# One product of layer 1 as a pair of row tiles in the middle of the layer: a layer norm, edge sum and MLP kernel on one Trainium2 core

## The chip, the cores and the metric

The kernel runs on one core of one Trainium2 chip, and the metric is the device time in microseconds of one execution. The engines are TensorE (PE in the profile, PEld its weight loads), VectorE (DVE), ScalarE (ACT), GpSimd (POOL) and SyncE (SP), which issues the DMAs. Each has its own stream of instructions; they meet at semaphores.

## The reference

12,500 nodes have 128 features each, and 200,000 edges, sorted by their destination, have 48. All is float32.

```
h    = relu(layernorm(x))
agg  = segment_sum(edge_attr, dst, 12500)          # 48 per node
c    = concat([h, agg], axis=1)                    # 176 per node
c    = silu(c @ W1 + b1)                           # W1: 176 x 256
c    = silu(c @ W2 + b2)                           # W2: 256 x 256
out  = x + h + c @ W3 + b3                         # W3: 256 x 128
```

## The kernel before

The nodes are worked on in NT = 28 tiles of 448 nodes (TILE); the last has 404. The MLP is computed with the features on the partitions and the nodes as columns, so a matmul of layers 1 and 2 has 448 columns. Layer 1 and 2 have 256 outputs, which are M = 2 blocks of 128, each in a PSUM bank of its own (`z[:, 0]` and `z[:, 1]`); both layers use the same two banks.

Layers 1 and 2 are computed in fp32r, a shorter form of float32. Each operand is therefore split in a high part, rounded to fp32r, and the rest, its low part, and three products are summed: high by high, low by high, high by low. For the node features that is L1054 to L1056. The edge sums have 48 rows only. Their high part lies in rows 0 to 47 of `agg_hilo` and their low part in rows 64 to 111 (ROW2 = 64), so one matmul of 112 rows with `w1e_hi`, which stands in both places, does two of the three products (L1059). The third one, W1's low part by the high part of the sums, is L1060: it takes the same 112 rows of `agg_hilo`, and `w1e_lo` is zero in all rows but 0 to 47. Layer 1 of a tile is thus five matmuls for each bank, ten in all.

The edges are summed per node by matmuls with a one-hot tile (`sum_tile`): each has 128 edges on the rows, 48 columns of weights (the edge features) and 42 columns of output. They come in pairs in different column tiles of the array: L1024 writes partitions 0 to 47 of `agg_ps`, L1027 partitions 64 to 111 of `stage`. A tile of nodes has 28 such pairs for each half of its groups, 56 in all.

The order on each engine is written out by hand. In step i TensorE does, one behind the other:

- layer 2 of tile i-2 (L1074 to L1078), which waits for h1_hi and h1_lo of that tile,
- layer 1 of tile i-1 (L1054 to L1060); the first matmul of each bank waits until ScalarE has read layer 2's sums out of it (semaphore `s_h2`), and L1059 of the first bank for the low part of the edge sums (`s_agg_lo`),
- the edge sums of tile i+1 (L1024, L1027),
- layer 3 of tile i-2 (L1092), then the transposes of tile i's normalized features (L1038).

ScalarE does in step i: `split_agg(i-1)` (L534, the high part of the sums), `stage_sums(i)` (L489), `relu(i-1)` (L528), `activate2(i-2, 0)` (L552, the Silu of layer 2's first bank), the clearing of a bank (L466), `activate2(i-2, 1)`, `activate1(i-1)` (L560 and L564, twice), the seeding of z3 with b3 (L541) and `normalize(i)` (L520, four pieces). VectorE does the sum of the agg parts (L849), the low parts (L859, L866, L873), the one-hot tiles (L705), the statistics and the output. GpSimd adds the staged sums (L443) and computes rstd.

Before the loop VectorE makes the low parts of the weights (`weights_lo`, L723), three subtractions; layer 1 of tile 0 waits for them (`s_w_lo`).

Of the kernel before, what the change touches and what calls it, by code (L numbers as in the profile page):

```python
# [26 lines left out]
ACT = mybir.ActivationFunctionType  # L27
AX = mybir.AxisListType
F32 = mybir.dt.float32
F32R = mybir.dt.float32r  # L30
# [3 lines left out]
def gnn_kernel(nc, x, dst, edge_attr, W1, b1, W2, b2, W3, b3, out):  # L34
    N, D = x.shape
    E, ED = edge_attr.shape
    HID = W1.shape[1]
    P = 128
    M = HID // P
    EPS = 1e-5  # L40

    PER = 4
# [6 lines left out]
    TILE = NPG * GPT  # L49
    TP = TILE // PER  # L50
    NT = -(-N // TILE)
# [11 lines left out]
    ROW2 = 64  # L63
# [23 lines left out]
    def nodes_p(t):  # L87
        return LAST_P if isinstance(t, int) and t == NT - 1 else TP

    with ExitStack() as ctx:  # L90
        def sb(name, shape, dt=F32):
            return ctx.enter_context(nc.sbuf_tensor(name, shape, dt))

        def ps(name, shape, dt=F32):
            return ctx.enter_context(nc.psum_tensor(name, shape, dt))

        def sem(name):
            return ctx.enter_context(nc.semaphore(name))


        w1x_hi = sb("w1x_hi", [D, HID], F32R)
        w1x_lo = sb("w1x_lo", [D, HID], F32R)
        w1e_hi = sb("w1e_hi", [ROW2 + ED, HID], F32R)
        w1e_lo = sb("w1e_lo", [ROW2 + ED, HID], F32R)
# [52 lines left out]
        hT_hi = sb("hT_hi", [D, TILE], F32R)  # L157
        hT_lo = sb("hT_lo", [D, TILE], F32R)
        agg = sb("agg", [ED, TILE])
        agg_hilo = sb("agg_hilo", [ROW2 + ED, TILE], F32R)  # L160
        h = sb("h", [P, 2 * M, TILE])
        h1, h2 = h[:, 0:M], h[:, M:2 * M]
        h1_hi = sb("h1_hi", [P, M, TILE], F32R)
# [8 lines left out]
        w1e_in = load_w[0:ROW2 + ED, (M + 1) * HID:(M + 2) * HID]  # L172
# [13 lines left out]
        z = ps("z", [P, M, BANK])  # L186
# [44 lines left out]
        s_agg = sem("agg_ready")  # L231
        s_agg_hi = sem("agg_hi_ready")
        s_agg_lo = sem("agg_lo_ready")
        s_w_hi = sem("weights_hi_ready")
        s_w_lo = sem("weights_lo_ready")
        s_carried = sem("overhang_carried")
# [7 lines left out]
        s_xn = sem("xn_ready")  # L244
# [5 lines left out]
        s_z1 = sem("z1_ready")  # L250
# [4 lines left out]
        s_h2 = sem("h2_ready")  # L255
# [6 lines left out]
        def wait(eng, s, count):  # L262

            if isinstance(count, int) and count <= 0:
                return
            eng.wait_ge(s, count)
# [21 lines left out]
        def has(i, lag, count):  # L288

            return not isinstance(i, int) or 0 <= i - lag < count  # L290

        def slot_turn(i, slot, slots=2):

            return (i - slot) // slots + 1
# [169 lines left out]
        def _(act):  # L464
            def clear_bank(k):
                act.activation(agg_ps[0:ED, k, :], zeros[0:ED, :].broadcast_to([ED, BANK]),  # L466
                               ACT.Copy).then_inc(s_clear, 1)
# [16 lines left out]
            def stage_sums(t, parity):  # L484

                act.wait_ge(s_summed, t + 1)
                if not isinstance(t, int) or t > 1:
                    act.wait_ge(s_added, added(t - 1))
                act.activation(staged[:, parity].rearrange("d k w -> d (k w)"),  # L489
                               stage[ROW2:ROW2 + ED, 0:STAGED],  # L490
                               ACT.Copy).then_inc(s_staged, 1)
# [16 lines left out]
            for a in (0, ROW2):  # L508
                act.activation(w1e_hi[a:a + ED, :], w1e_in[a:a + ED, :], ACT.Copy).then_inc(s_w_hi, 1)

            def normalize(i, turn):

                np_ = nodes_p(i)
                parity = turn % 2
                act.wait_ge(s_x[turn], 16 * slot_turn(i, turn, XSLOTS) + (16 if np_ != TP else 0))
                act.wait_ge(s_nmr, i + 1)
                wait(act, s_tp, i - 1)
                wait(act, s_plain, i - 1)
                for q in range(PER):
                    ln = act.activation(xn[0:np_, parity, q, :], x_t[0:np_, turn, q, :], ACT.Identity,  # L520
                                        bias=nmr[0:np_, parity, q:q + 1], scale=rstd[0:np_, parity, q:q + 1])
                ln.then_inc(s_xn, 1)

            def relu(t):
                n = PER * nodes_p(t)
                act.wait_ge(s_tp, t + 1)
                wait(act, s_z1, M * t)
                act.activation(hT_hi[:, 0:n], tp[:, 0:n], ACT.Relu).then_inc(s_hT, 1)  # L528

            def split_agg(t):  # L530
                n = PER * nodes_p(t)
                act.wait_ge(s_agg, t + 1)
                wait(act, s_z1, M * t)
                act.activation(agg_hilo[0:ED, 0:n], agg[:, 0:n], ACT.Copy).then_inc(s_agg_hi, 1)  # L534

            def seed_b3(t):

                np_ = nodes_p(t)
                act.wait_ge(s_begun, 1)
                wait(act, s_out, t)  # L540
                act.activation(z3[0:np_, :, :], b3r[0:np_, :].unsqueeze(1).broadcast_to([np_, PER, D]),  # L541
                               ACT.Copy).then_inc(s_seeded, 1)
# [23 lines left out]
            def step(i, turn):  # L566
                parity = turn % 2
                if has(i, 1, NT):
                    split_agg(i - 1)
                if has(i, 0, NT) and not (isinstance(i, int) and i == 1):  # L570
                    stage_sums(i, parity)
                if has(i, 1, NT):
                    relu(i - 1)
                last = isinstance(i, int) and i >= NT - 1
                if last and i == NT + 1:
                    seed_b3(i - 2)
                if has(i, 2, NT):
                    activate2(i - 2, 0)
                if last and i <= NT:
                    seed_b3(i - 2)  # L580
                if has(i, 1, NT - 2):
                    act.wait_ge(s_carried, i)
                    clear_bank(1 - parity)
                if has(i, 2, NT):
                    activate2(i - 2, 1)
                if has(i, 1, NT):
                    activate1(i - 1)
                if has(i, 2, NT) and not last:
                    seed_b3(i - 2)
                if has(i, 0, NT) and not (isinstance(i, int) and i == NT - 1):  # L590
                    normalize(i, turn)
                if isinstance(i, int) and i == NT - 2:
                    normalize(i + 1, (turn + 1) % XSLOTS)

            clear_carry(2)
            normalize(0, 0)
            stage_sums(1, 1)
            pipeline(act, step)

        @block.vector  # L600
        def _(dve):
# [113 lines left out]
            def weights_lo():  # L715
                dve.wait_ge(s_w_hi, 4)
                dve.wait_ge(s_pool_zero, 4)
                for lo, whole, hi in (
                        (w2_lo[:, :, :].rearrange("p m n -> p (m n)"), w2_in.rearrange("p m n -> p (m n)"),
                         w2_hi[:, :, :].rearrange("p m n -> p (m n)")),  # L720
                        (w1x_lo[:, :], w1x_in, w1x_hi[:, :]),
                        (w1e_lo[0:ED, :], w1e_in[0:ED, :], w1e_hi[0:ED, :])):
                    dve.tensor_tensor(lo, whole, hi.bitcast(F32), ALU.subtract).then_inc(s_w_lo, 1)  # L723

            dve.wait_ge(s_small0T, 1)
# [213 lines left out]
        def _(pe):  # L939
# [102 lines left out]
            def layer1(t):  # L1042

                n = PER * nodes_p(t)
                pe.wait_ge(s_hT_lo, t + 1)
                if isinstance(t, int) and t == 0:
                    pe.wait_ge(s_w_lo, 3)
                    pe.wait_ge(s_w_hi, 4)
                    pe.wait_ge(s_weights, WEIGHTS)
                    pe.wait_ge(s_const, CONSTS)  # L1050
                for m in range(M):
                    cols = slice(m * P, (m + 1) * P)
                    wait(pe, s_h2, M * (t - 1) + m + 1)
                    pe.matmul(z[:, m, 0:n], w1x_hi[:, cols], hT_hi[:, 0:n], start=True, stop=False)  # L1054
                    pe.matmul(z[:, m, 0:n], w1x_lo[:, cols], hT_hi[:, 0:n], start=False, stop=False)  # L1055
                    pe.matmul(z[:, m, 0:n], w1x_hi[:, cols], hT_lo[:, 0:n], start=False, stop=False)  # L1056
                    if m == 0:
                        pe.wait_ge(s_agg_lo, t + 1)
                    pe.matmul(z[:, m, 0:n], w1e_hi[:, cols], agg_hilo[:, 0:n], start=False, stop=False)  # L1059
                    pe.matmul(z[:, m, 0:n], w1e_lo[:, cols], agg_hilo[:, 0:n],  # L1060
                              start=False, stop=True).then_inc(s_z1, 1)

            def layer2(t, b):

# [64 lines left out]
            for c in range(FULL_ROWS):  # L1129
                pe.matmul(invalid_sum[:, 0:1], g["invalid"][:, c:c + 1], one[:, :],  # L1130
                          start=(c == 0), stop=(c == FULL_ROWS - 1))
            pe.matmul(invalid_sum[:, 1:2], g["invalid"][0:LAST_G, FULL_ROWS:ROWS], one[0:LAST_G, :],
                      start=True, stop=True, skip_group_check=True).then_inc(s_smallT, 1)
# [26 lines left out]
```

## Time and profile before

| | |
|---|---|
| median of 3 runs | 301.86 us (301.55 to 302.54) |
| the profiled execution's own time | 301.52 us |
| its span, first to last instruction | 299.8 us |
| busy share of the span: PE, PEld, DVE, ACT, POOL | 94%, 86%, 83%, 76%, 38% |
| mean granted TensorE clock | 0.983 |

All durations of the trace are from that one execution. Matmuls are pipelined: the record of one overlaps that of the next, and their ends are modelled, so the distance of the starts tells what one costs. The idle time of an engine that isn't the bound costs nothing.

### The profile page before, as it was taken

The page shows a single profiled execution, that of the slowest core. Times are in us where ns is not written, and L with a number is a line of the kernel's source. Part 1 is how long each engine was busy: PE and PEld are TensorE (multiplying, and loading weights), DVE is VectorE, ACT ScalarE, POOL GpSimd, SP SyncE. Part 2 cuts the span into 40 slices and gives each one's busy share as a digit, 9 for nine tenths or more (in the row PEclk, how much of TensorE's full clock was granted, in tenths as well). Part 3 has the DMA queues.
Part 4 walks back from the last instruction along what each step waited for, and adds up shares of the span by engine and source line. Part 5 has one row for each costly group of instructions (what it writes and reads, how often), then busy time and mean ns, then how long its engine had stood idle before and what let it go on. Part 6 is the DMA issues. An engine that isn't in the chain of part 4 may idle for free.

```text
span 299.8 us, 12214 instructions
## 1 busy us (share of the span) xinstructions
PE 282.7 (94%) x4378; PEld 258.8 (86%) x4379; DVE 249.6 (83%) x617; ACT 229.3 (76%) x435; POOL 113.8 (38%) x241
## 2 busy tenths in 40 slices
PE   6791998999999999999999999999999999999995
PEld 5681888899999999999999999999999999999794
DVE  7878897799888998889988898889988889875551
ACT  8773586787788877888778887888777887789662
POOL 3053554243433435334353334434444343532200
PEclk9888799999999999999999999999999999999999
DMA  6999076368655686557855678556875568731112
GB/s 164 303 286 254 4 218 181 94 191 245 209 155 159 215 245 191 157 151 235 245 170 150 178 237 237 158 156 184 244 230 159 147 200 245 205 104 33 33 32 58
DMA packets 79226, 52.94 MB, mean 177 GB/s; under 512 B 2949, under 2 KB 78815, under 8 KB 79205
## 3 DMA queue, kind: packets, MB, share of 16 engines
q1 hardware_dynamic: 79205, 52.70, 61.0%
q8 instruction: 8, 0.13, 0.2%
q14 instruction: 13, 0.11, 0.1%
HBM read 46.29 MB, written 6.40 MB: 176 GB/s over the span
## 4 chain that ended last, share of the span: by engine, by line
PE 81%; issue 5%; ACT 3%; DVE 3%; DMA 2%; POOL 2%; SPq 1%; POOLq 0%; ACTq 0%; DVEq 0%
PE agg_ps L1024 19%; PE z L1092 17%; PE z L1074 7%; PE z L1078 7%; PE z L1075 7%; PE z L1054 4%; PE stage L1027 4%; PE z L1056 4%; PE z L1059 4%; PE z L1060 4%; PE z L1055 4%; PE tp L1038 3%; DMA raw<-in_edge_attr_dram 2%; POOL agg_carry L443 2%; ACT xn L520 1%
## 5 line engine op out<-in xcount | busy, mean ns | idle before, releaser
L443 POOL TENSOR_TENSOR agg_carry<-staged,agg_carry 48x42 f32 x196 | 71.8, 366 | 90.8 <-ACT staged L489 61.2
L1024 PEld LDWEIGHTS agg_ps<-onehot,raw 128*48 128x48 f32 x1560 | 73.2, 126 | 9.4 <-issue 9.4
L1027 PE MATMUL stage<-onehot,raw 128*48 128x42 f32 x1568 | 77.2, 215 | 3.2 <-DMA raw<-in_edge_attr_dram 1.9
L705 DVE TENSOR_TENSOR onehot<-window,rel 128x1176 f32<-128x1176 f32 (+1 forms) x57 | 76.9, 1351 | 3.9 <-DVE stats L680 2.7
L1024 PE MATMUL agg_ps<-onehot,raw 128*48 128x42 f32 x1560 | 77.0, 215 | 0.0
L1027 PEld LDWEIGHTS stage<-onehot,raw 128*48 128x48 f32 x1568 | 73.6, 126 | 3.0 <-issue 3.0
L426 POOL TENSOR_TENSOR rstd<-vareps,minus_half 112x4 f32<-112x4 f32 (+1 forms) x28 | 38.8, 1384 | 75.9 <-DVE vareps L690 75.9
L1092 PE MATMUL z<-w,h 128*112 128x128 f32 (+1 forms) x448 | 55.9, 278 | 0.8 <-ACT h L552 0.8
L1092 PEld LDWEIGHTS z<-w,h 128*112 128x112 f32 (+1 forms) x448 | 50.4, 176 | 2.4 <-ACT z L548 1.1
L552 ACT ACTIVATE h<-z,b2c 128x448 f32<-128x448 f32 (+1 forms) x56 | 35.5, 634 | 20.0 <-PE z L1078 17.2
L520 ACT ACTIVATE xn<-x_t,nmr,rstd 112x128 f32<-112x128 f32 (+1 forms) x112 | 45.6, 478 | 0.5 <-DVE nmr L698 0.5
L560 ACT ACTIVATE h<-z,b1c 128x448 f32<-128x448 f32 (+1 forms) x56 | 35.0, 626 | 14.0 <-PE z L1060 14.0
L1074 PE MATMUL z<-h_hi,w_hi 128*128 128x448 f32 (+1 forms) x112 | 43.2, 386 | 0.0
L1075 PE MATMUL z<-h_hi,w_lo 128*128 128x448 f32 (+1 forms) x112 | 40.9, 365 | 0.0
L873 DVE TENSOR_TENSOR h_lo<-h,h_hi 128x448 fp32r<-128x448 f32 (+1 forms) x56 | 34.9, 623 | 6.5 <-ACT h_hi L564 4.9
L849 DVE TENSOR_TENSOR agg<-agg_ps,agg_carry 48x448 f32<-48x448 f32 (+1 forms) x28 | 17.2, 615 | 19.8 <-PE stage L1027 18.9
L564 ACT ACTIVATE h_hi<-h 128x448 fp32r<-128x448 f32 (+1 forms) x56 | 32.3, 576 | 1.8
L1078 PE MATMUL z<-h_lo,w_hi 128*128 128x448 f32 (+1 forms) x112 | 31.8, 365 | 0.0
L1054 PE MATMUL z<-hT_hi,w1x_hi 128*128 128x448 f32 (+1 forms) x56 | 21.3, 381 | 6.6 <-DVE hT_lo L866 6.0
L534 ACT ACTIVATE agg_hilo<-agg 48x448 fp32r<-48x448 f32 (+1 forms) x28 | 16.0, 573 | 13.4 <-DVE agg L849 13.4
L680 DVE BATCH_NORM_STATS2 stats<-x_t 112x6 f32<-112x128 f32 (+1 forms) x112 | 24.2, 278 | 0.0
L1078 PEld LDWEIGHTS z<-h_lo,w_hi 128*128 128x128 f32 x112 | 21.1, 188 | 1.8
(122 smaller groups left out, 427.5 us busy)
## 6 DMA issues: line engine op xcount, KB each, us to landing
raw<-in_edge_attr_dram SPq DMA_DIRECT2D x55, 672.0 KB, 6.0
x_t<-in_x_dram SPq DMA_DIRECT2D x27, 224.0 KB, 6.1
out_dram<-out_t SPq DMA_DIRECT2D x27, 224.0 KB, 6.0
dst_rows<-in_dst_dram SPq DMA_DIRECT2D x1, 512.0 KB
raw<-in_edge_attr_dram SPq DMA_DIRECT2D x1, 288.0 KB, 3.5
dst_rows<-in_dst_dram SPq DMA_DIRECT2D x1, 256.0 KB, 2.7
out_t<-in_L_gnn_W_dram SPq DMA_DIRECT2D x1, 256.0 KB, 7.3
x_t<-in_x_dram SPq DMA_DIRECT2D x1, 192.0 KB
```

What stands on the lines that cost most here:

```text
L426: pool.tensor_tensor(rstd[0:np_, parity], vareps[0:np_, :], minus_half[0:np_, :], ALU.pow).then_inc(s_rstd, 1)
L443: pool.tensor_tensor(into, staged[:, parity, n, :], into, ALU.add).then_inc(s_added, 1)
L520: ln = act.activation(xn[0:np_, parity, q, :], x_t[0:np_, turn, q, :], ACT.Identity, bias=nmr[0:np_, parity, q:q + 1], scale=rstd[0:np_, p ...
L552: act.activation(h2[:, m, 0:n], z[:, m, 0:n], ACT.Silu, bias=b2c[:, m:m + 1]).then_inc(s_h2, 1)
L560: act.activation(h1[:, m, 0:n], z[:, m, 0:n], ACT.Silu, bias=b1c[:, m:m + 1]).then_inc(s_h1, 1)
L705: return dve.tensor_tensor(onehot[:, slot, at * PER:n * PER, :], window[:, :].unsqueeze(1).broadcast_to([P, cols_n, WINDOW]), cols.unsquee ...
L1024: mm = pe.matmul(banks[0:ED, bass.ds(offsets[at - first], WINDOW)], edges, into, start=False, stop=True, skip_group_check=True, tile_posit ...
L1027: mm = pe.matmul(stage[ROW2:ROW2 + ED, at * WINDOW:(at + 1) * WINDOW], edges, into, start=(at == 0 and j == 0), stop=True, skip_group_chec ...
L1074: pe.matmul(z[:, m, 0:n], w2_hi[:, k, cols], h1_hi[:, k, 0:n], start=(k == 0), stop=False)
L1075: pe.matmul(z[:, m, 0:n], w2_lo[:, k, cols], h1_hi[:, k, 0:n], start=False, stop=False)
L1078: mm = pe.matmul(z[:, m, 0:n], w2_hi[:, k, cols], h1_lo[:, k, 0:n], start=False, stop=(k == M - 1))
L1092: mm = pe.matmul(into[0:np_], h2[:, k, q * np_:(q + 1) * np_], w3[:, k, :], start=False, stop=(k == M - 1), skip_group_check=True)
```

## The change

For all tiles but the last, the two L1060 matmuls (one for each bank) are replaced by two matmuls of 48 rows each, which are placed one behind the other in the middle of the layer. The first, at rows 0 to 47 (tile position (0, 0)), closes the first bank's sum. The second, at rows 64 to 111 (tile position (64, 0)), opens the second bank's, so that its L1054 no longer has `start=True`, and L1059 closes that bank. The second needs the sums' high part in rows 64 to 111, so ScalarE writes another copy of it (`agg_hi_again`, tile `agg_hi_below`), behind relu, and VectorE writes `w1e_lo` there too. TensorE waits for that copy, and for both banks, ahead of the pair. The parameter `quarters` of `normalize` and the variable `first` change nothing in what is issued. The last tile keeps its two full matmuls; rows 64 to 111 of its `w1e_lo` are no longer zero, so that it adds the product of the two low parts as well.

```diff
@@ weights_lo @@
-                        (w1e_lo[0:ED, :], w1e_in[0:ED, :], w1e_hi[0:ED, :])):
+                        (w1e_lo[0:ED, :], w1e_in[0:ED, :], w1e_hi[0:ED, :]),
+                        (w1e_lo[ROW2:ROW2 + ED, :], w1e_in[ROW2:ROW2 + ED, :], w1e_hi[ROW2:ROW2 + ED, :])):
@@ ScalarE @@
+            def agg_hi_again(t):
+                n = PER * nodes_p(t)
+                act.wait_ge(s_agg, t + 1)
+                wait(act, s_z1, M * t)
+                act.activation(agg_hi_below[ROW2:ROW2 + ED, 0:n], agg[:, 0:n], ACT.Copy).then_inc(s_agg_below, 1)
...
                 if has(i, 1, NT):
                     relu(i - 1)
...
+                if has(i, 1, NT - 1):
+                    agg_hi_again(i - 1)
@@ layer1 @@
+                last = isinstance(t, int) and t == NT - 1
                 pe.wait_ge(s_hT_lo, t + 1)
                 if isinstance(t, int) and t == 0:
-                    pe.wait_ge(s_w_lo, 3)
+                    pe.wait_ge(s_w_lo, 4)
...
                 for m in range(M):
                     cols = slice(m * P, (m + 1) * P)
                     wait(pe, s_h2, M * (t - 1) + m + 1)
-                    pe.matmul(z[:, m, 0:n], w1x_hi[:, cols], hT_hi[:, 0:n], start=True, stop=False)
+                    pe.matmul(z[:, m, 0:n], w1x_hi[:, cols], hT_hi[:, 0:n], start=(m == 0 or last), stop=False)
...
-                    pe.matmul(z[:, m, 0:n], w1e_hi[:, cols], agg_hilo[:, 0:n], start=False, stop=False)
-                    pe.matmul(z[:, m, 0:n], w1e_lo[:, cols], agg_hilo[:, 0:n],
-                              start=False, stop=True).then_inc(s_z1, 1)
+                    mm = pe.matmul(z[:, m, 0:n], w1e_hi[:, cols], agg_hilo[:, 0:n],
+                                   start=False, stop=(m == 1 and not last))
+                    if m == 1 and not last:
+                        mm.then_inc(s_z1, 1)
+                    if last:
+                        pe.matmul(z[:, m, 0:n], w1e_lo[:, cols], agg_hilo[:, 0:n],
+                                  start=False, stop=True).then_inc(s_z1, 1)
+                    elif m == 0:
+                        pe.wait_ge(s_agg_below, t + 1)
+                        wait(pe, s_h2, M * (t - 1) + 2)
+                        pe.matmul(z[:, 0, 0:n], w1e_lo[0:ED, 0:P], agg_hilo[0:ED, 0:n],
+                                  start=False, stop=True, tile_position=(0, 0)).then_inc(s_z1, 1)
+                        pe.matmul(z[:, 1, 0:n], w1e_lo[ROW2:ROW2 + ED, P:2 * P], agg_hi_below[ROW2:ROW2 + ED, 0:n],
+                                  start=True, stop=False, tile_position=(ROW2, 0))
```

## Rows read from the trace of the kernel before

**Rows 1.** The page: granted TensorE clock in 40 slices; ScalarE's copy L534 (busy, mean ns).

```profile
PEclk9888799999999999999999999999999999999999
...
L534 ACT ACTIVATE agg_hilo<-agg 48x448 fp32r<-48x448 f32 (+1 forms) x28 | 16.0, 573 | 13.4 <-DVE agg L849 13.4
```

**Rows 2.** The page: the chain that ended last, by engine.

```profile
PE 81%; issue 5%; ACT 3%; DVE 3%; DMA 2%; POOL 2%; SPq 1%; POOLq 0%; ACTq 0%; DVEq 0%
```

**Rows 3.** That chain in time order, 140 to 175 us: start, us, what.

```profile
146.93 0.20 PE z L1054
...
156.41 0.20 PE z L1054
...
158.86 0.04 PE agg_ps L1024
```

**Rows 4.** Waits of TensorE: us in total, times, longest.

```profile
PE z L1054 <- DVE hT_lo L866: 6.0, 2, 5.6
...
PE z L1054 <- ACT h L552: 0.6, 1, 0.6
```

**Rows 5.** Timeline of TensorE's matmuls, layer 1 into the edge sums: start, us.

```profile
156.86 0.36 PE L1059 MATMUL z<-agg_hilo,w1e_hi 112*128 112x448 f32 x1
...
157.28 0.37 PE L1054 MATMUL z<-hT_hi,w1x_hi 128*128 128x448 f32 x1
...
157.90 0.37 PE L1059 MATMUL z<-agg_hilo,w1e_hi 112*128 112x448 f32 x1
158.10 0.36 PE L1060 MATMUL z<-agg_hilo,w1e_lo 112*128 112x448 f32 x1
158.39 0.24 PE L1024 MATMUL agg_ps<-onehot,raw 128*48 128x42 f32 x1
158.40 0.24 PE L1027 MATMUL stage<-onehot,raw 128*48 128x42 f32 x1
```

**Rows 6.** Timeline of the weight loads in the same stretch.

```profile
157.14 0.19 PEld L1054 LDWEIGHTS z<-hT_hi,w1x_hi 128*128 128x128 f32 x1
...
157.90 0.19 PEld L1060 LDWEIGHTS z<-agg_hilo,w1e_lo 112*128 112x128 f32 x1
158.39 0.12 PEld L1024 LDWEIGHTS agg_ps<-onehot,raw 128*48 128x48 f32 x1 [0.30 <-issue]
```

**Rows 7.** Timeline, the edge sums into layer 3.

```profile
151.42 0.21 PE L1027 MATMUL stage<-onehot,raw 128*48 128x42 f32 x1
151.56 0.17 PEld L1092 LDWEIGHTS z<-w,h 128*112 128x112 f32 x1
```

**Rows 8.** Timeline, the first matmuls of layer 2.

```profile
153.69 0.19 PEld L1074 LDWEIGHTS z<-h_hi,w_hi 128*128 128x128 f32 x1
153.80 0.19 PEld L1075 LDWEIGHTS z<-h_hi,w_lo 128*128 128x128 f32 x1
154.00 0.37 PE L1075 MATMUL z<-h_hi,w_lo 128*128 128x448 f32 x1
```

**Rows 9.** Timeline near the start: transposes of 128 rows, then of 7.

```profile
16.80 0.39 PE L947 MATMUL z<-ident,rel_rows 128*128 128x128 f32 x2
...
16.91 0.28 PE L947 MATMUL z<-ident,rel_rows 128*128 128x128 f32 x1
17.11 0.19 PEld L947 LDWEIGHTS tp<-ident,rel_rows 7*128 7x128 f32 x1
```

**Rows 10.** The chain in time order, 21 to 34 us.

```profile
22.92 0.34 DVE w1e_lo L723
...
31.22 0.37 PE z L1060
```

**Rows 11.** Layer 1 of tile 0 as a window: us, engines busy (x), granted clock, DMA.

```profile
29.40:34.50 5.10, 5.10 (x12) 3.76 (x12) 5.07 (x9) 2.18 (x4) 3.74 (x4) 0.56 0.03 8
```

**Rows 12.** Timeline of ScalarE, layer 2's second Silu.

```profile
156.45 0.64 ACT L552 ACTIVATE h<-z,b2c 128x448 f32<-128x448 f32 x1
```

**Rows 13.** Waits of ScalarE: us in total, times, longest.

```profile
ACT h L552 <- PE z L1078: 17.2, 25, 0.7
```

More of the change, by code:

```diff
@@ L160, in gnn_kernel @@
         agg_hilo = sb("agg_hilo", [ROW2 + ED, TILE], F32R)
+        agg_hi_below = sb("agg_hi_below", [ROW2 + ED, TILE], F32R)
         h = sb("h", [P, 2 * M, TILE])
@@ L233, in gnn_kernel @@
         s_agg_lo = sem("agg_lo_ready")
+        s_agg_below = sem("agg_hi_below_ready")
         s_w_hi = sem("weights_hi_ready")
@@ L509, in _, with normalize @@
                 act.activation(w1e_hi[a:a + ED, :], w1e_in[a:a + ED, :], ACT.Copy).then_inc(s_w_hi, 1)
-            def normalize(i, turn):
+            def normalize(i, turn, quarters=range(PER)):
                 np_ = nodes_p(i)
@@ L518, in normalize @@
                 wait(act, s_plain, i - 1)
-                for q in range(PER):
+                for q in quarters:
                     ln = act.activation(xn[0:np_, parity, q, :], x_t[0:np_, turn, q, :], ACT.Identity,
                                         bias=nmr[0:np_, parity, q:q + 1], scale=rstd[0:np_, parity, q:q + 1])
-                ln.then_inc(s_xn, 1)
+                if quarters[-1] == PER - 1:
+                    ln.then_inc(s_xn, 1)
             def relu(t):
@@ L573, in step @@
                     relu(i - 1)
+                first = isinstance(i, int) and i == 1
                 last = isinstance(i, int) and i >= NT - 1
+                if has(i, 1, NT - 1):
+                    agg_hi_again(i - 1)
                 if last and i == NT + 1:
```

## The prediction

> **What bounds the kernel now.** I read the page first: TensorE's granted clock is full in all slices but the first few [rows 1]. A high busy share alone wouldn't make it the bound, so the chain that ended last came next: 81% of it is TensorE [rows 2]. In time order, in the middle of the run [rows 3], it is nothing but matmuls. One tile takes 9.48 us there (L1054 at 146.93 and at 156.41). The waits of TensorE say the same from the other side: for h it waits once, 0.6 us, and the large wait, 5.6 us for hT_lo, is at the start [rows 4]. So whatever the stream of TensorE gains or loses in layer 1 arrives in the end in full, 27 times (28 tiles, the last keeps its old form). ScalarE and VectorE matter only where they would come late for TensorE.
>
> The records of matmuls are 0.36 us long and overlap; what a matmul costs is the distance of starts, 0.20 us for 448 columns, with its weight load beside the matmul ahead of it [rows 5, 6]: the load for L1060 starts at 157.90, with L1059's matmul.
>
> **The change part by part.** Removed: in each of 27 tiles the two full L1060 matmuls. Added: one pair of 48-row tiles, at rows 0 and 64, in different banks. If the pair runs as one matmul, and nothing else changes, a tile saves one step of 0.20 us.
>
> But the pair stands between full matmuls, and the trace shows what happens where the shape in use changes. From L1060 (full) to L1024 (tiles of 48 columns): the weights aren't loaded beside the last full matmul; the load starts at 158.39, 0.29 behind that matmul's start at 158.10, where 0.20 would be the end of its columns [rows 5, 6]. The other way, L1027 to L1092: load at 151.56, 0.14 behind a start whose own columns take some 0.04 [rows 3, 7]. So either way costs 0.09 to 0.10 us of nothing, and then the weight load lies bare. Its price: at 153.69 and 153.80 two loads of 128 columns follow one another at 0.11, and the second matmul then starts at 154.00, 0.20 behind the second load [rows 8]; a bare load costs 0.11. Are tiles of rows like that too? The nearest row is the transposes of 7 rows near the start: the last one with 128 rows starts at 16.91, the load for the first with 7 rows at 17.11, 0.20 later, although the 128-row ones stand 0.11 apart, 16.80 to 16.91 [rows 9]. That is the same gap of 0.09. I take that a pair of 64-row tiles pays it on entry and on exit. The Trainium skill (TensorEngine Tiling (Array Packing), Key Properties) says that a change of tiling mode, unlike a change of tile, drains TensorE; by that rule the gap is paid twice here, as in my sum. By the speedup of up to 2x that the same page gives for a contraction of 64 or less (Theoretical Speedup) alone, a tile would save its 0.20 us, 5.3 us in 26 tiles. The trace agrees with the drain for tiles of columns (0.09) and shows no 64-row tile.
>
> The sum for a tile at full clock, from L1059's start (m = 0) to the start proper of L1054 (m = 1): 0.29 to the pair's weight load; 0.11 for the load; 0.01 by which the second tile stands behind the first (L1024 and L1027 start 0.01 apart [rows 5]; at most 0.11, if the two loads go one after the other); 0.29 from the pair's start to the next full weight load, as at L1060; 0.11 for that load. Together 0.81. Before it is 0.42 (156.86 to 157.28). That is 0.39 more, and L1060 of m = 1 is gone, 0.21 less: **+0.18 us a tile**, with the serial loads +0.28, and 0.31 if the dispatch behind a semaphore adds the 0.03 by which L1054's load stands further ahead of its matmul after a wait (157.14 to 157.28 [rows 5, 6]). 26 tiles give 4.7 us (to 8.1).
>
> The 27th is tile 0. Its matmuls run at a granted clock of 0.56, that is mostly at the lower of the two levels, 1.2 GHz, behind a wait of 5.6 us, and stand 0.37 apart [rows 4, 10, 11]. If all terms double, it costs 0.36 (to 0.6).
>
> VectorE gets one more w1e_lo subtraction (48x256) at the start. It lies on the chain there: 0.34 us for the same instruction, between w1x_lo and the one-hot tile, and the chain goes on over VectorE to hT_lo, for which TensorE waits [rows 10]. **+0.34 us**, once; nothing covers it.
>
> ScalarE gets one more copy (agg_hi_again) in each of 27 tiles, behind relu; the same copy, L534, takes 0.57 us [rows 1]. Queued behind it are both Silus of layer 2 (L552), the clearing of the bank, layer 1's Silus and xn. The cover is the idle time ahead of the first L552: 17.2 us in 25 waits over the run, 0.69 each [rows 13]. The copy's 0.57 fits in with 0.1 to spare, so it costs nothing, and 0.58 a tile if that cover were gone. The wait for the copy (s_agg_below) is over some 2 us before the pair.
>
> The pair also waits for h2's second bank, as L1054 (m = 1) did. That Silu ends at 157.09 and L1054's load follows at 157.14 [rows 6, 12], so today this wait is only just met. The pair's load comes at 157.15 by the sum, so it is met by 0.01; I put nothing, at worst 0.03 (above). What is late next is the first Silu of layer 1, which starts some 0.2 us later, with the pair; ScalarE has the growth of TensorE's own step to make that up. The drain of sums, the carry and the loads follow TensorE.
>
> Sum: 4.7 + 0.36 + 0.34 = 5.4 us. The profiled execution took 301.52 us for its span of 299.8 (1.7 lie around it), so 306.9; the median of the three runs stands 0.34 higher, which gives 307.3. I say 307.2.
>
> **Rivals.**
> (A) The forecast: pair concurrent, both drains and both loads bare. 306.5 to 310.5, the upper end with serial loads: 26 x 0.31 + 0.6 + 0.34 = 9.0 above 301.52. Chance 0.60.
> (B) The pair isn't concurrent: the second tile streams behind the first, for 0.20 more. Tile 0.38, so 9.9 + 0.76 + 0.34 = 11.0 and 312.6. Against it: the column tiles start in pairs 0.01 apart at 0.04 a pair [rows 3, 5]. For it: those are 42 columns long, and no pair of 448 columns is to be seen. Chance 0.18. Its kin, a cover on ScalarE that fails, would be as dear; 0.02 of this.
> (C) The entry is free: the first tile's weights load beside L1059's matmul, and only the exit drains. Then a tile is 0.21 + 0.01 + 0.29 + 0.11 = 0.62 against 0.42 + 0.21, nothing; with 0.34 for VectorE the time is 301.9 to 302.3. By the Trainium skill (TensorE: Matmul & The Clock Gate, The mechanism) a weight load aimed at row groups that nothing in flight uses may go ahead of the matmul in flight; L1059 uses 112 rows, so the rule doesn't quite reach, and the trace shows the opposite at L1024. Chance 0.10.
> (D) The other side: a change between full and row tiles costs nothing (the drain belongs to column tiles, and the 7-row gap has another cause), so the pair takes one step of 0.20. It decides as soon as entry and exit together cost under 0.20 a tile beyond a full matmul. 26 x 0.20 + 0.37 - 0.34 = 5.2 faster, 296.5. For it: tile rows and columns may differ; against it: [rows 9]. Chance 0.12.
>
> **How the numbers follow.** About 0.3% (0.9 us) is what a measurement of this kernel can tell from no change. Slower: A and B, 0.78, with a little of C, 0.80. Same: 0.08. Faster: D, 0.12. The range leaves out D and the upper edge of B: 301.9 to 312.6; the likeliest case's own is 306.5 to 310.5.
>
> **What the changed profile would show.** One load of weights for the pair 0.29 behind L1059's matmul, the next full one 0.4 behind that; matmuls of the pair 0.01 apart (right) or 0.1 to 0.2 apart (serial loads, B). The distance from L1059 to the second L1054 is 0.8 instead of 0.42; a tile takes 9.66 us instead of 9.48. Idle ahead of the first L552 shrinks to 0.1 to 0.3 and no wait of TensorE for h appears in the steady tiles. hT_lo of tile 0 comes 0.34 later. What would make it wrong: a load for the pair at 0.20 behind L1059 (C or D), or a tile of 9.28.

## The result, and the profile after

The changed kernel takes 308.61 us (median of 4 runs, 307.72 to 309.50) against 301.71 us (4 runs), a ratio of 1.024 with a 95% interval of 1.018 to 1.030: 6.9 us slower. The profiled execution took 309.5 us for a span of 307.8 us, where the one of before had 299.8. All ratios and medians of this document rest on fast runs, with one execution of `pair_twice` at 405.73 us the only slow one.

The page, engines and the chain that ended last [rows 1, 2]:

```profile
PE 289.0 (94%) x4378; PEld 252.9 (82%) x4379; DVE 251.1 (82%) x618; ACT 245.0 (80%) x462; POOL 114.8 (37%) x241
...
PEclk9796699999999999999999999999999999999999
...
PE 82%; DVE 6%; issue 4%; ACT 4%; POOL 2%; POOLq 0%; ACTq 0%; DVEq 0%
```

The number of matmuls is the same, and so is the granted clock outside the start; from 28 to 52 us it is 0.84 on the mean here and 0.88 before. TensorE still carries the chain. Its weight loads are 6 us less busy (252.9 us) although their number is the same: busy time counts loads that lie beside each other once, and those of the pair do, as do the two behind it (below). In time order, 140 to 175 us [rows 3]:

```profile
151.26 0.20 PE z L1068
...
160.98 0.20 PE z L1068
...
161.59 0.20 PE z L1073
161.80 0.43 PE z L1083
162.27 0.40 PE z L1068
...
163.28 0.17 PE agg_ps L1037
```

A tile takes 9.72 us (151.26 to 160.98) instead of 9.48. (L1068 is L1054 of before, L1073 is L1059; L1083 and L1085 are the pair.) All of the growth is in two steps: the pair and the full matmul behind it. The timelines of matmuls and of weight loads say what is in them [rows 5, 6]:

```profile
161.43 0.36 PE L1073 MATMUL z<-agg_hilo,w1e_hi 112*128 112x448 f32 x1
161.80 0.43 PE L1083 MATMUL z<-agg_hilo,w1e_lo 48*128 48x448 f32 x1
161.80 0.47 PE L1085 MATMUL z<-agg_hi_below,w1e_lo 48*128 48x448 f32 x1
162.20 0.47 PE L1068 MATMUL z<-hT_hi,w1x_hi 128*128 128x448 f32 x1
162.51 0.37 PE L1069 MATMUL z<-hT_hi,w1x_lo 128*128 128x448 f32 x1
```

```profile
161.77 0.18 PEld L1083 LDWEIGHTS z<-agg_hilo,w1e_lo 48*128 48x128 f32 x1 [0.35 <-issue]
161.80 0.18 PEld L1085 LDWEIGHTS z<-agg_hi_below,w1e_lo 48*128 48x128 f32 x1
162.19 0.19 PEld L1068 LDWEIGHTS z<-hT_hi,w1x_hi 128*128 128x128 f32 x1 [0.21 <-issue]
162.30 0.19 PEld L1069 LDWEIGHTS z<-hT_hi,w1x_lo 128*128 128x128 f32 x1
```

The reader is to see three things. The pair's two matmuls start together. Their first weight load starts 0.34 behind L1073's start (161.43 to 161.77), and the full weight load behind them 0.42 after that. And both loads lie bare, behind the columns of the matmul ahead of them and not beside them, with idle stretches of the load stream of 0.35 and 0.21 in front. ScalarE [rows 12], whose second Silu ends at 161.65:

```profile
159.13 0.58 ACT L543 ACTIVATE agg_hi_below<-agg 48x448 fp32r<-48x448 f32 x1
159.79 0.64 ACT L561 ACTIVATE h<-z,b2c 128x448 f32<-128x448 f32 x1
...
161.02 0.63 ACT L561 ACTIVATE h<-z,b2c 128x448 f32<-128x448 f32 x1
```

The new copy L543 lies in the idle time it was meant for. Both Silus stand where they stood against TensorE: the second starts 0.04 behind L1068 of the first bank (161.02 and 160.98), as before (156.45 and 156.41 [rows 3, 12]). The chain at the start [rows 10], first two lines of before, then the changed kernel's:

```profile
20.20 1.00 POOL rstd L426
...
29.36 0.74 PE z L1054
```

```profile
20.73 1.00 POOL rstd L428
...
23.44 0.34 DVE w1e_lo L736
...
23.81 0.42 DVE w1e_lo L736
...
30.46 0.74 PE z L1068
```

The fourth subtraction takes 0.42 us, on the chain. From rstd to layer 1 it is 9.16 us before (20.20 to 29.36) and 9.73 here (20.73 to 30.46): the start is 0.57 longer. The other 0.53 by which layer 1 begins later lies ahead of the subtraction: rstd itself starts anywhere between 19.70 and 21.10 in the profiles of this study, with the change or without it.

### The profile page after: what moved, and what is told of

The parts are those of the page before. It is cut to its first block, busy times and chain, and to the rows that moved or that the text cites. A ratio compares the mean times of both kernels' runs of the same rounds, so it can differ in the third digit from the quotient of the medians.

```text
span 307.8 us, 12294 instructions
## 1 busy us (share of the span) xinstructions
PE 289.0 (94%) x4378; PEld 252.9 (82%) x4379; DVE 251.1 (82%) x618; ACT 245.0 (80%) x462; POOL 114.8 (37%) x241
## 4 chain that ended last, share of the span: by engine, by line
PE 82%; DVE 6%; issue 4%; ACT 4%; POOL 2%; POOLq 0%; ACTq 0%; DVEq 0%
PE agg_ps L1037 18%; PE z L1117 16%; PE z L1099 6%; PE z L1103 6%; PE z L1100 6%; PE z L1068 5%; PE stage L1040 4%; PE z L1083 4%; PE z L1069 4%; PE z L1073 4%; PE z L1070 4%; PE tp L1051 3%; POOL agg_carry L445 2%; ACT xn L522 1%; DVE onehot L717 1%
## 5 line engine op out<-in xcount | busy, mean ns | idle before, releaser
L445 POOL TENSOR_TENSOR agg_carry<-staged,agg_carry 48x42 f32 x196 | 72.8, 371 | 95.0 <-ACT staged L491 65.4
L1040 PE MATMUL stage<-onehot,raw 128*48 128x42 f32 x1568 | 76.3, 214 | 1.4 <-issue 1.1
L1037 PE MATMUL agg_ps<-onehot,raw 128*48 128x42 f32 x1560 | 76.2, 214 | 1.5 <-DVE onehot L717 1.5
L1040 PEld LDWEIGHTS stage<-onehot,raw 128*48 128x48 f32 x1568 | 72.8, 125 | 1.8 <-issue 1.8
L569 ACT ACTIVATE h<-z,b1c 128x448 f32<-128x448 f32 (+1 forms) x56 | 35.0, 625 | 19.1 <-PE z L1083 18.3
L561 ACT ACTIVATE h<-z,b2c 128x448 f32<-128x448 f32 (+1 forms) x56 | 35.4, 632 | 5.7 <-PE z L1103 0.7
L1068 PE MATMUL z<-hT_hi,w1x_hi 128*128 128x448 f32 (+1 forms) x56 | 24.1, 430 | 7.3 <-DVE hT_lo L879 6.1
L1068 PEld LDWEIGHTS z<-hT_hi,w1x_hi 128*128 128x128 f32 x56 | 10.7, 191 | 14.7 <-DVE hT_lo L879 8.2
```

What stands on the lines that cost most here:

```text
L445: pool.tensor_tensor(into, staged[:, parity, n, :], into, ALU.add).then_inc(s_added, 1)
L561: act.activation(h2[:, m, 0:n], z[:, m, 0:n], ACT.Silu, bias=b2c[:, m:m + 1]).then_inc(s_h2, 1)
L1037: mm = pe.matmul(banks[0:ED, bass.ds(offsets[at - first], WINDOW)], edges, into, start=False, stop=True, skip_group_check=True, tile_posit ...
L1040: mm = pe.matmul(stage[ROW2:ROW2 + ED, at * WINDOW:(at + 1) * WINDOW], edges, into, start=(at == 0 and j == 0), stop=True, skip_group_chec ...
```

## The experiments

Each ratio is to the kernel before, run beside it on the same chip. "Tile" is the distance between starts of layer 3's first matmul in the chain, averaged over 3 to 13 tiles between 130 and 280 us; by the same count it is 9.48 us before and 9.72 changed.

| run | ratio (95%) | us over before, medians | tile, us |
|---|---|---|---|
| the change | 1.024 (1.018 to 1.030) | 6.9 | 9.72 |
| copies_alone | 1.003 (1.001 to 1.005) | 1.1 | 9.48 |
| one_after_the_other | 1.041 (1.039 to 1.043) | 12.5 | 9.89 |
| copy_wait_first | 1.018 (1.015 to 1.020) | 5.4 | 9.64 |
| pair_at_end | 1.071 (1.068 to 1.074) | 21.3 | 10.41 |
| single_in_the_middle | 1.036 (1.032 to 1.039) | 10.1 | 9.85 |
| single_at_the_end | 1.021 (1.015 to 1.026) | 6.5 | 9.66 |
| pair_twice | 1.040 (1.036 to 1.044) | 11.9 | 9.93 |
| order_alone | 1.022 (1.018 to 1.026) | 7.1 | 9.71 |
| order_copy_wait_first | 1.018 (1.015 to 1.022) | 5.6 | 9.64 |
| full_at_end | 1.048 (1.044 to 1.052) | 14.6 | 10.02 |
| own_bank_full | 1.000 (0.998 to 1.002) | 0.2 | 9.46 |
| own_bank_pair | 1.016 (1.013 to 1.018) | 5.0 | 9.64 |

The medians of the kernel before lie between 301.30 and 302.14 us from one experiment to the next, so the tile, from the profile, tells more than the last microsecond. Wherever an experiment on the changed kernel has full matmuls of 112 rows for the pair, they add the product of the two low parts as well, since `w1e_lo` is filled in both places.

### Is it TensorE's shapes, or ScalarE's copy?

**copies_alone**: everything added on ScalarE and VectorE stays, TensorE has its ten full matmuls in the old order.

```diff
-                    pe.matmul(z[:, m, 0:n], w1x_hi[:, cols], hT_hi[:, 0:n], start=(m == 0 or last), stop=False)
+                    pe.matmul(z[:, m, 0:n], w1x_hi[:, cols], hT_hi[:, 0:n], start=True, stop=False)
...
-                    elif m == 0:
-                        pe.wait_ge(s_agg_below, t + 1)
-                        wait(pe, s_h2, M * (t - 1) + 2)
-                        pe.matmul(z[:, 0, 0:n], w1e_lo[0:ED, 0:P], ... tile_position=(0, 0)).then_inc(s_z1, 1)
-                        pe.matmul(z[:, 1, 0:n], w1e_lo[ROW2:ROW2 + ED, P:2 * P], ... tile_position=(ROW2, 0))
+                    if m == 0 and not last:
+                        pe.wait_ge(s_agg_below, t + 1)
+                    pe.matmul(z[:, m, 0:n], w1e_lo[:, cols], agg_hilo[:, 0:n],
+                              start=False, stop=True).then_inc(s_z1, 1)
```

> The changed kernel's extra ScalarE copy, its wait and VectorE's fourth subtraction stay, but layer 1 has its ten full matmuls again (as a side effect the product of the two low parts is added). Theory (the cost lies in the two changes of shape on TensorE): 0.3 to 0.5 us above the kernel before, from the subtraction at the start alone (it took 0.42 in the profile of the changed kernel), and a tile of 9.48 us. Rival (the added copy takes ScalarE's slack and makes TensorE late): most of the 6.9 us is still there, a tile takes about 9.7 us.

Measured: 1.003, and a tile of 9.48 us. ScalarE's copy costs nothing; what is left is 0.9 us by the ratio (its interval is 0.4 to 1.5), somewhat more than the 0.3 to 0.5 expected. The start accounts for 0.57 of it: from rstd to layer 1 this profile too has 9.73 us (21.10 to 30.83). The rest is within the interval.

**one_after_the_other**: the second matmul of the pair uses rows 0 to 47 and `agg_hilo` too.

```diff
-                        pe.matmul(z[:, 1, 0:n], w1e_lo[ROW2:ROW2 + ED, P:2 * P], agg_hi_below[ROW2:ROW2 + ED, 0:n],
-                                  start=True, stop=False, tile_position=(ROW2, 0))
+                        pe.matmul(z[:, 1, 0:n], w1e_lo[0:ED, P:2 * P], agg_hilo[0:ED, 0:n],
+                                  start=True, stop=False, tile_position=(0, 0))
```

> Both 48-row matmuls of the pair at rows 0 to 47, so they can't run side by side. Theory (the changed kernel's pair is concurrent, starts 0.003 us apart in its profile): the second costs its own 0.19 to 0.20 us, 27 times, 5.1 to 5.5 us above the changed kernel, some 12 us above the kernel before; tile 9.91 us. Rival (the pair is serial already, and only its records overlap): as the changed kernel, within 1 us.

Measured: 0.18 us a tile over the changed kernel (9.89), 5.6 us by the medians, as the theory had it. Timeline of its matmuls, to be held against the changed kernel's:

```profile
164.62 0.44 PE L1083 MATMUL z<-agg_hilo,w1e_lo 48*128 48x448 f32 x1
164.90 0.36 PE L1085 MATMUL z<-agg_hilo,w1e_lo 48*128 48x448 f32 x1
165.20 0.47 PE L1068 MATMUL z<-hT_hi,w1x_hi 128*128 128x448 f32 x1
```

The starts are 0.28 apart here and 0.00 there. The pair at rows 0 and 64 is truly concurrent, which disposes of rival B of the prediction.

**pair_twice**: the pair is issued twice (the second adds its product once more).

```diff
+                        for again in range(2):
+                            mm = pe.matmul(z[:, 0, 0:n], ..., stop=(again == 1), tile_position=(0, 0))
...
+                            pe.matmul(z[:, 1, 0:n], ..., start=(again == 0), stop=False, tile_position=(ROW2, 0))
```

> The changed kernel with the pair issued twice in a row (the second adds the same product once more, so the output has twice W1's low part by the sums' high part). Theory (between tiles of rows nothing drains, and a pair runs as one matmul): 0.19 to 0.20 us a tile above the changed kernel, tile 9.92 us, 5.2 us. Rival 1 (the next weights of tiles of rows aren't loaded ahead): 0.30 us a tile, 8 us. Rival 2 (a change between tiles of one mode drains too): 0.5 us a tile, over 13 us.

Measured: 0.21 us a tile over the changed kernel, 9.93. Timeline of the weight loads:

```profile
162.86 0.18 PEld L1084 LDWEIGHTS z<-agg_hilo,w1e_lo 48*128 48x128 f32 x1 [0.35 <-issue]
162.90 0.18 PEld L1088 LDWEIGHTS z<-agg_hi_below,w1e_lo 48*128 48x128 f32 x1
162.97 0.19 PEld L1084 LDWEIGHTS z<-agg_hilo,w1e_lo 48*128 48x128 f32 x1
163.00 0.19 PEld L1088 LDWEIGHTS z<-agg_hi_below,w1e_lo 48*128 48x128 f32 x1
```

The second pair's weights are loaded 0.11 behind the first's, ahead of their turn. So inside the mode a further pair costs the 0.20 of one matmul: the rest is paid at the borders.

### What one change of shape costs by itself

**single_in_the_middle** and **single_at_the_end**: the kernel before, with one of its two L1060 on 48 rows instead of 112, in the same place. Nothing else is touched on any engine.

```diff
+                    rows = ED if m == 0 else ROW2 + ED          # m == 1 for single_at_the_end
-                    pe.matmul(z[:, m, 0:n], w1e_lo[:, cols], agg_hilo[:, 0:n],
+                    pe.matmul(z[:, m, 0:n], w1e_lo[0:rows, cols], agg_hilo[0:rows, 0:n],
```

> The kernel before with one edit: the first bank's L1060 has 48 rows instead of 112 (the other 64 are zero rows of the weights), in the same place, so no matmul is added or taken away, and nothing on the other engines. Theory (a 48-row matmul between full ones pays a drain and a bare weight load twice): from L1059 to the second L1054's own start 0.29 + 0.40 + 0.11 = 0.80 instead of 0.42, 0.38 us a tile, tile 9.86 us, 10.5 us above the kernel before. Rival (what costs in the changed kernel is the pair, its two banks or its second weight load, not the shape): within 1 us of the kernel before.

> As the one before, but the second bank's L1060 alone has 48 rows, right in front of the edge sums. Theory (it adds one change of shape, rows to columns, which costs what full to columns costs): 0.29 + 0.11 + 0.29 = 0.69 instead of 0.49, 0.20 us a tile, 5.5 us above the kernel before. Rival (a change from tiles of rows to tiles of columns drains nothing): 0.1 us a tile, 3 us. The 21 us of pair_at_end are then not the shape's: there the first Silu of layer 1 is a microsecond later.

Measured: 0.37 us a tile in the middle and 0.18 at the end; 0.38 and 0.20 were expected. A matmul with fewer rows makes the kernel 10 us slower. The loads, in the middle (L1061 is L1060 of before):

```profile
161.47 0.19 PEld L1059 LDWEIGHTS z<-agg_hilo,w1e_hi 112*128 112x128 f32 x1
161.97 0.18 PEld L1061 LDWEIGHTS z<-agg_hilo,w1e_lo 48*128 48x128 f32 x1 [0.31 <-issue]
162.37 0.19 PEld L1054 LDWEIGHTS z<-hT_hi,w1x_hi 128*128 128x128 f32 x1 [0.22 <-issue]
```

and at the end, where the edge sums' tiles of columns follow:

```profile
161.95 0.18 PEld L1061 LDWEIGHTS z<-agg_hilo,w1e_lo 48*128 48x128 f32 x1 [0.31 <-issue]
162.35 0.12 PEld L1024 LDWEIGHTS agg_ps<-onehot,raw 128*48 128x48 f32 x1 [0.21 <-issue]
```

0.40 us from load to load in both: rows to columns costs what rows to full costs. The rival of a cheap change from rows to columns falls.

### The wait for h2, which the drain had hidden

**copy_wait_first**: only the place of one wait differs from the changed kernel.

```diff
+                if not last:
+                    pe.wait_ge(s_agg_below, t + 1)
                 pe.wait_ge(s_hT_lo, t + 1)
...
                     elif m == 0:
-                        pe.wait_ge(s_agg_below, t + 1)
                         wait(pe, s_h2, M * (t - 1) + 2)
```

> The changed kernel with the wait for the second copy moved from in front of the pair to the head of layer 1, where it is long fulfilled; the pair waits for h2's second bank alone. The pair's weights are loaded 0.335 us behind L1073 in the changed kernel's profile, where 0.29 was the drain alone. Theory (two waits in front of the pair need an instruction of their own, which starts only when h2 is there): the distance falls to about 0.29, 0.045 us a tile, 1.2 us in all. Rival (the load is late because of h2 itself, whatever stands beside it): no change, within 0.3 us.

Measured: 0.08 us a tile less than the changed kernel (9.64). Timelines of matmul and load:

```profile
169.35 0.36 PE L1075 MATMUL z<-agg_hilo,w1e_hi 112*128 112x448 f32 x1
169.64 0.47 PE L1084 MATMUL z<-agg_hilo,w1e_lo 48*128 48x448 f32 x1
...
169.64 0.18 PEld L1084 LDWEIGHTS z<-agg_hilo,w1e_lo 48*128 48x128 f32 x1 [0.31 <-ACT h L561]
169.64 0.18 PEld L1086 LDWEIGHTS z<-agg_hi_below,w1e_lo 48*128 48x128 f32 x1
170.04 0.19 PEld L1070 LDWEIGHTS z<-hT_hi,w1x_hi 128*128 128x128 f32 x1 [0.22 <-issue]
```

The distance to the load is 0.29, and the second load now starts with the first. Two waits in front of one instruction thus cost 0.05 at the entry and 0.03 at the second load, the size that the theory gave. But the trace names "ACT h" as what ended the idle time here, not the drain, and that raised the question of which of them it is.

**order_alone** and **order_copy_wait_first**: as the changed kernel and as copy_wait_first, with two full matmuls of 112 rows for the pair, one behind the other. No shape changes any more.

```diff
-                        pe.matmul(z[:, 0, 0:n], w1e_lo[0:ED, 0:P], agg_hilo[0:ED, 0:n], ... tile_position=(0, 0))
-                        pe.matmul(z[:, 1, 0:n], w1e_lo[ROW2:ROW2 + ED, P:2 * P], agg_hi_below[...], ... tile_position=(ROW2, 0))
+                        pe.matmul(z[:, 0, 0:n], w1e_lo[:, 0:P], agg_hilo[:, 0:n],
+                                  start=False, stop=True).then_inc(s_z1, 1)
+                        pe.matmul(z[:, 1, 0:n], w1e_lo[:, P:2 * P], agg_hilo[:, 0:n],
+                                  start=True, stop=False)
```

> The changed kernel's order and waits, but the pair's two matmuls are full ones of 112 rows, one after the other (the first tile's product of the two low parts comes with it). Theory (the changed kernel's loss is the change of shape; the wait for h2's second bank, one matmul earlier now, lay beside the drain there and lies bare here): L1073 to the pair's load 0.33 instead of 0.20 for lack of h2, 0.1 us a tile, 2 to 3.5 us above the kernel before. Rival (the order alone costs what the changed kernel costs): 6 to 7 us above it.

> order_alone (two full matmuls of 112 rows in the pair's place) with the wait for the second copy at the head of the layer, as in copy_wait_first. Theory (the two matmuls wait for h2's second bank, whose Silu ends 0.22 us behind L1075's start there, and the separate semaphore instruction is gone): the load comes 0.27 us behind L1075, not 0.33 and not 0.20; with the bare load a tile takes 9.63 to 9.65 us, 0.15 more than before; 4.5 us above the kernel before. That is what copy_wait_first measured with the pair of 48 rows: the pair saves one matmul and its exit eats it. Rival (without the separate instruction the wait is as good as met, as the kernel before has it): 9.5 us a tile, within 1 us.

Measured: 7.1 us over before for order_alone. The expectation was 2 to 3.5, so the theory as it stood then, that the change of shape makes the loss, failed: the order with no change of shape costs what the changed kernel costs (9.71 and 9.72 us a tile). Its loads:

```profile
162.32 0.19 PEld L1083 LDWEIGHTS z<-agg_hilo,w1e_lo 112*128 112x128 f32 x1 [0.34 <-issue]
162.43 0.19 PEld L1085 LDWEIGHTS z<-agg_hilo,w1e_lo 112*128 112x128 f32 x1
162.63 0.19 PEld L1068 LDWEIGHTS z<-hT_hi,w1x_hi 128*128 128x128 f32 x1
```

and the Silu that they wait for:

```profile
161.57 0.64 ACT L561 ACTIVATE h<-z,b2c 128x448 f32<-128x448 f32 x1
```

That Silu ends at 162.21, the load follows 0.11 later. With the copy's wait moved away (order_copy_wait_first) the Silu ends at 160.06, and the load follows 0.05 later:

```profile
160.11 0.19 PEld L1084 LDWEIGHTS z<-agg_hilo,w1e_lo 112*128 112x128 f32 x1 [0.28 <-ACT h L561]
```

The distance from L1075's start to the load is 0.27 (159.84 to 160.11) and a tile takes 9.64 us, the same as with the pair. The second wait is thus worth 0.06 by itself (0.11 against 0.05 behind the Silu); copy_wait_first showed only 0.05 of it, since there the drain holds the load until 0.29. My error in the expectation of order_alone was arithmetic: beside the 0.13 of waiting, the bare load costs 0.11, and that is 0.24 a tile, 6.4 us.

**own_bank_full** and **own_bank_pair**: these two take the wait away without a race. Layer 1's second block is summed in the eighth PSUM bank, which the kernel had free, so its opening needn't wait until layer 2's sums are read.

```diff
+        z_own = ps("z_own", [P, BANK])
+        z1 = (z[:, 0, :], z_own[:, :])
...
-                    wait(pe, s_h2, M * (t - 1) + m + 1)
+                    if m == 0:
+                        wait(pe, s_h2, M * (t - 1) + 1)
...
-                        wait(pe, s_h2, M * (t - 1) + 2)
```

> order_copy_wait_first (the changed kernel's order with full matmuls of 112 rows) where layer 1's second block is summed in a PSUM bank of its own, which the kernel had free, so that nothing in front of the pair waits for h2's second bank. Theory (the order costs only through that wait): 9.46 to 9.48 us a tile, 0 to 1 us above the kernel before. Rival (something else in the order costs, such as the earlier opening or the later first Silu): 9.64 us a tile, 4.5 us above.

> The same with the changed kernel's pair of 48-row matmuls: no wait for h2 in front of it, only the change of shape is left. Theory (drain at entry and wait for h2 lie beside each other in the changed kernel, and either alone sets the pair back to 0.27 to 0.29 us): the load still comes 0.29 us behind L1059's successor in the layer, a tile takes 9.64 to 9.65 us, 4.5 to 5.5 us above the kernel before, and 4.5 above own_bank_full. Rival (the loss is all the wait for h2, and the drain is nothing while the array is busy anyway): 9.44 us a tile or less, no slower than before.

Measured: 1.000 (9.46 us a tile) with full matmuls, 1.016 (9.64 us) with the pair. Matmul and loads of the latter:

```profile
150.68 0.36 PE L1078 MATMUL z<-agg_hilo,w1e_hi 112*128 112x448 f32 x1
...
150.97 0.18 PEld L1086 LDWEIGHTS z<-agg_hilo,w1e_lo 48*128 48x128 f32 x1 [0.31 <-issue]
...
151.37 0.19 PEld L1073 LDWEIGHTS z_own<-hT_hi,w1x_hi 128*128 128x128 f32 x1 [0.22 <-issue]
```

With no wait, the pair's load still comes 0.29 behind the full matmul. And from own_bank_full to own_bank_pair it is 0.18 us a tile, the prediction's figure for the change of shape. So both causes are real, and at the entry they lie side by side: the drain ends 0.29 behind L1073's start, the wait at 0.34 with the copy's wait beside it (changed kernel, order_alone) and at 0.27 without. In the changed kernel it is therefore the wait that ends last, by 0.05. Take one away and the other holds the place. Only with both gone is the order free.

### The pair where the shape changes anyway

**pair_at_end** puts the pair behind the second bank's L1073, so that it closes both banks; **full_at_end** puts two full matmuls there.

```diff
-                    elif m == 0:
+                    elif m == 1:
                         pe.wait_ge(s_agg_below, t + 1)
-                        wait(pe, s_h2, M * (t - 1) + 2)
                         pe.matmul(z[:, 0, 0:n], ..., start=False, stop=True, tile_position=(0, 0)).then_inc(s_z1, 1)
-                        pe.matmul(z[:, 1, 0:n], ..., start=True, stop=False, tile_position=(ROW2, 0))
+                        pe.matmul(z[:, 1, 0:n], ..., start=False, stop=True, tile_position=(ROW2, 0)).then_inc(s_z1, 1)
```

> The pair closes both banks at the end of layer 1, in front of the edge sums, where the shape changes anyway. Theory (each change of shape costs a drain of 0.09 and a bare weight load): from the second L1059 to the edge sums' first load it is 0.29 + 0.11 + 0.01 + 0.29 = 0.70, against 0.20 + 0.29 and the 0.20 of the first bank's full matmul before: no difference but the 0.4 us at the start, so 0.2 to 0.9 us above the kernel before, 6 below the changed one. Rival 1 (rows to columns costs more than full to columns, both switches are paid again): 2 to 4 us above the kernel before. Rival 2 (what costs is the late wait for h2, gone here): 5 us below the kernel before.

> pair_at_end with two full matmuls of 112 rows instead of the pair: no change of shape is added, the first bank is still closed only at the end. Theory (pair_at_end's 21 us are ScalarE's: its first Silu of layer 1 comes 0.9 us later behind an idle stretch of 1.56 us, and the chain of copies, Silus and normalization then ends too late for TensorE): 18 to 22 us above the kernel before, a tile of 10.1 to 10.4 us on the mean. Rival (the change from tiles of rows to tiles of columns behind the pair costs it): within 2 us of the kernel before.

Measured: 21.3 and 14.6 us over before. Both expectations missed: pair_at_end's theory and both rivals by over 15 us, full_at_end's by 3.4. On TensorE the borders came out as summed (the pair's load 0.29 behind L1073, the next one 0.40 behind that). What the sum lacked is, first, the wait for h2 again: four matmuls and not five now stand in front of the second bank's L1068, so that it comes early enough to meet the wait. In full_at_end its load starts 0.28 behind L1073's start (162.37):

```profile
162.65 0.19 PEld L1068 LDWEIGHTS z<-hT_hi,w1x_hi 128*128 128x128 f32 x1 [0.29 <-ACT h L561]
```

From layer 1's first matmul to the edge sums it is 2.14 us before, 2.31 in full_at_end and 2.30 in pair_at_end (means of 14 tiles in the middle of the run): 0.17 a tile or 4.6 us in 27, and the same with the pair as with full matmuls. What it lacked second is ScalarE. The chain of full_at_end in time order:

```profile
163.73 0.22 PE z L1080
163.95 0.02 issue
163.98 0.64 ACT h L569
...
166.26 0.59 ACT z L550
166.85 0.04 issue
166.89 2.00 PE z L1114 x16
```

The first Silu of layer 1 (L569) waits for the first bank, which is closed a whole half of the layer later; ScalarE stands idle for 1.38 us ahead of it, its queue of Silus and copies ends late, and layer 3 (L1114) now waits for the seeding of z3 (L550). With the pair the same waits add up to 6.9 us, from the waits of TensorE in pair_at_end:

```profile
PE z L1114 <- ACT z L550: 6.9, 23, 0.3
```

Part of the 6.7 us between the two runs fits the later close: from L1073's start to the Silu it is 0.80 us with the pair (167.13 to 167.93) and 0.61 with full matmuls (163.37 to 163.98), 0.19 more, and from the edge sums to layer 3 it is 2.65 us before, 2.82 with full matmuls and 3.02 with the pair, 0.20 more, 5.4 us in 27. That the one makes the other is worked out, not tried by itself. The rest of both losses lies in layer 2, from its first matmul to the next layer 1: 2.53 us before, 2.72 and 2.92 here, mostly as a stretch ahead of its second bank in every second tile. What sets that stretch isn't shown.

## Why the prediction was right, point by point

The forecast was 307.2 us, slower; 308.6 was measured, in the range and in the likeliest case's own.

- **The bound.** Right: TensorE's step grows by 0.24 us in each of 22 tiles in a row (9.72 for 9.48), and from the first layer 1 to the last it is 6.9 us more (265.8 for 258.9). By the prediction's count, 26 tiles, the step gives 6.2.
- **Both drains, both bare loads.** Right, and shown without the pair: 0.37 and 0.18 us a tile for a single 48-row matmul, where the terms 0.29, 0.40 and 0.11 give 0.38 and 0.20. With the wait gone the pair costs 0.18 (own_bank_pair over own_bank_full), as summed. In the changed kernel only the exit is the drain's; at the entry the wait for h2 ends 0.05 behind the drain. That the entry's term of 0.29 comes close there is luck: it stands for a wait that the sum put at nothing, and that happens to end where the drain does.
- **The pair is concurrent.** Right (one_after_the_other), rival B falls. C and D fall with own_bank_pair and the single matmuls.
- **+0.18 us a tile.** Too small for the changed kernel, by 0.06: this is the mis-sized term. The step "I put nothing, at worst 0.03", for the waits in front of the pair, is 0.05 at the entry (0.34 for 0.29), and the second tile stands 0.03 behind instead of 0.01. Both go when the copy's wait is elsewhere (copy_wait_first, +0.16 a tile): then the sum holds. The sign "no wait of TensorE for h" failed too, though the list of waits hardly shows it (`PE z L1083 <- ACT h L561: 0.2, 1, 0.2`): the waits of the other tiles stand under "issue".
- **What the prediction missed** is a rival: that the order costs the same without any change of shape. It saw that the wait for h2 was met by 0.01 us in the shadow of the drain, and put it at nothing. It is nothing only beside the drain. The saving of one matmul, 0.20, is what the exit's drain and bare load eat; the entry's loss would be there with full matmuls too.
- **ScalarE's copy at nothing.** Right (copies_alone: a tile as before; ahead of layer 2's first Silu 0.08 us of idle time is left, 159.71 to 159.79).
- **+0.34 us at the start.** Too small: 0.57 from rstd to layer 1, of which 0.45 is the new subtraction (23.81 to the one-hot tile at 24.26).
- **Tile 0, 0.36.** From 30.46 to 34.78 us, 4.32, against 29.36 to 33.46, 4.10: 0.22 more.

The sum with the measured terms is 6.2 + 0.22 + 0.57 = 7.0 us, against 6.9 between the medians. So close a fit is more than these runs can vouch for. The profiles differ by 8.0 us, of which 0.53 lies ahead of rstd; and the first step alone, from layer 1 of tile 0 to that of tile 1, is 11.31 before and 12.10 changed, and goes with the granted clock of 28 to 52 us: 11.19 to 11.87 in the eight profiles that have 0.86 to 0.89 there, 12.10 to 13.19 in the six that have 0.79 to 0.84. Two of the prediction's sums are off in the last digit, B's (312.5) and D's (296.3); nothing hangs on them.

## What to carry to other kernels

A small matmul between full ones is not cheap: count a change of shape on each side (here 0.09 of drain and 0.11 of bare weight load), and pack tiles only where several follow one another. Where two shapes meet already, one pair costs TensorE nothing and gains nothing (2.30 us in pair_at_end, 2.31 in full_at_end). When a wait and a stall lie side by side, price each alone: an edit that removes one of them gains little or nothing, and an experiment that removes one alone can convict the wrong one. And before a matmul is moved to where it is cheaper for TensorE, ask which engine waits for the bank that it closes.

## What the runs showed of the hardware that was not expected

- A matmul on 48 rows is dearer than the same one on 112 rows with zeros, by 0.37 us between full matmuls; the drain shows for tiles of rows as for tiles of columns, 0.29 from start to load in every case with no wait. The Trainium skill (TensorEngine Tiling (Array Packing), Key Properties) has the drain, with no figure; these runs agree, and it ends 0.09 us behind the last column, if the 0.20 between the starts of full matmuls is taken for the columns. The speedup of up to 2x that the page gives for a contraction of 64 or less (Theoretical Speedup) is there too, but inside the mode alone: a second pair costs 0.21 us.
- Two semaphore waits in front of one matmul cost more than one, though the first had long been met: the weight load came 0.12 us behind the end of the Silu it waited for (161.65 to 161.77; 0.11 in order_alone), with the other wait elsewhere 0.05 (order_copy_wait_first). With the pair the tile fell by 0.08 us for it.
